# Stack loads in half as many transfers, and loads put in another order, in a two-layer decoder on one Trainium2 core

## What is computed

```python
x = ln(x + causal_attention(x))          # L0_attn
x = ln(x + cross_attention(x, ctx))      # L0_xattn: 1024 context tokens of 192 features per sequence
x = ln(x + soft_moe(x))                  # L0_ffn: 8 experts x 128 slots, 256 -> 1024 -> 256
x = ln(x + causal_attention(x))          # L1_attn
x = ln(x + cross_attention(x, ctx))      # L1_xattn
x = ln(x + block(x))                     # L1_ffn: own causal attention, then top-2 of 8 experts
```

## Time and profile before

| | us |
|---|---|
| median of 3 runs | 3067.17 (3059.79 to 3073.33) |
| profiled execution, its own time | 3064.33 |
| span of that execution, first to last instruction | 3062.5 |
| PE busy | 2568.9 |
| DVE busy | 1499.4 |
| ACT busy | 1346.1 |
| GpSimd busy | 457.8 |

### The profile page before, as it was taken

One profiled execution on the slowest core, in us unless ns is written; L12 is line 12 of the kernel. 1 busy time (PEld: TensorE's weight loads), 2 busy tenths in 40 slices (PEclk: granted clock), 3 DMA queues, 4 the chain that ended last, 5 costly groups with the idle time before them and its releaser, 6 DMA issues. The chain is left out here.

```text
span 3062.5 us, 48054 instructions
## 1 busy us (share of the span) xinstructions
PE 2568.9 (84%) x15793; PEld 1469.9 (48%) x15794; DVE 1499.4 (49%) x4196; ACT 1346.1 (44%) x2886; POOL 457.8 (15%) x719
## 2 busy tenths in 40 slices
PE   4999999999828979998588999898987986489992
PEld 2555544444314446676355544343434554356671
DVE  0555677888425420013444487777744564222223
ACT  2555456666634432211244456665754553022220
POOL 3222212101110000000112212212122000500004
PEclk7899999999969999999699999999998997599996
DMA  8344664454000012203644465354422332711102
GB/s 205 97 126 126 131 118 82 68 73 73 1 17 1 1 59 88 87 17 137 158 109 123 111 128 80 56 101 62 92 59 60 103 83 95 249 31 34 34 30 89
DMA packets 184550, 259.98 MB, mean 85 GB/s; under 512 B 32952, under 2 KB 106944, under 8 KB 184256
## 3 DMA queue, kind: packets, MB, share of 16 engines
q1 hardware_dynamic: 181264, 248.85, 34.5%
q0 software_dynamic: 3072, 8.39, 0.9%
HBM read 180.71 MB, written 81.53 MB: 86 GB/s over the span
## 5 line engine op out<-in xcount | busy, mean ns | idle before, releaser
L1345 ACT ACTIVATE second_p<-psum 128x512 f32<-128x512 f32 (+3 forms) x1024 | 461.7, 520 | 287.9 <-PE psum L1211 284.3
L1345 ACT ACTIVATE first_p<-psum 128x512 f32<-128x512 f32 (+3 forms) x768 | 365.7, 547 | 179.1 <-PE psum L1211 176.5
L1419 DVE TENSOR_REDUCE first_max_parts<-psum 128x1 f32<-128x512 f32 x512 | 323.0, 684 | 74.7 <-PE psum L1188 72.1
L1419 DVE TENSOR_REDUCE second_max_parts<-psum 128x1 f32<-128x512 f32 x512 | 321.9, 683 | 72.9 <-PE psum L1188 70.2
L1415 DVE CUSTOM_DVE_ANT_0 second_masked<-psum,mask_qk 128x384 f32<-128x384 f32 (+3 forms) x512 | 230.0, 489 | 230.7 <-PE psum L1188 189.1
L1201 PE MATMUL psum<-second_q,second_k 64*128 64x512 f32 (+3 forms) x1024 | 227.7, 440 | 42.1 <-DVE second_max_parts L1419 26.2
L1188 PE MATMUL psum<-second_k,second_q 64*128 64x512 f32 (+3 forms) x1024 | 203.7, 395 | 67.5 <-DMA second_k<-a_k_parts 51.5
L1223 PE MATMUL psum<-second_p,second_v_aug 128*32 128x512 f32 (+3 forms) x2048 | 240.1, 542 | 8.3 <-ACT second_p L1345 8.1
L1188 PE MATMUL psum<-first_k,first_q 64*128 64x512 f32 (+3 forms) x768 | 158.0, 411 | 61.7 <-ACT first_held L1382 26.0
L1201 PEld LDWEIGHTS psum<-second_q,second_k 64*128 64x128 f32 x1024 | 98.8, 188 | 230.1 <-issue 83.6
L1415 DVE CUSTOM_DVE_ANT_0 first_masked<-psum,mask_qk 128x128 f32<-128x128 f32 (+3 forms) x256 | 114.8, 488 | 179.7 <-PE psum L1188 152.5
(11 more groups left out here) (317 smaller groups left out, 3819.2 us busy)
## 6 DMA issues: line engine op xcount, KB each, us to landing
first_k<-c_k_parts SPq DMA_DIRECT2D x128, 128.0 KB, 5.7
second_q<-a_q_parts SPq DMA_DIRECT2D x256, 64.0 KB, 2.8
second_k<-a_k_parts SPq DMA_DIRECT2D x256, 64.0 KB, 2.9
second_k<-c_k_parts SPq DMA_DIRECT2D x128, 128.0 KB, 5.6
first_q<-a_q_parts SPq DMA_DIRECT2D x128, 64.0 KB, 2.9
first_k<-a_k_parts SPq DMA_DIRECT2D x128, 64.0 KB, 2.9
c_k_parts<-first_held SPq DMA_DIRECT2D x16, 512.0 KB, 3.2
first_q<-c_q_parts SPq DMA_DIRECT2D x128, 64.0 KB, 5.3
```

Of the source, the lines that this page charges most:

```text
L1345: evacuated(act.activation(probs[tile % 2][:, 2 * h + p, q0:SEQ], bank[:, q0:SEQ], ACT.Exp, scale=scale), event)
L1419: evacuated(v.reduce_max(max_parts[n % 2][:, h, p, qt, k0 // BANK:k0 // BANK + 1], bank[:, 0:width], axis=AX_X), event)
```

## The change

Three things. First, a stack is loaded in 8 transfers: one fills two blocks, that is 32 partitions. To make the two heads of a partition contiguous in DRAM, the columns of the q and k weights and biases are reordered on the host (`by_heads`), so that row 2d + i holds feature d of head i; a partition's run is then 2 x 512 or 2 x 1024 tokens in one piece. For q both blocks hold the same part, so the DRAM side repeats its 16 rows twice; for k the two blocks hold parts 0 and 1. `keys_of` views a causal stack's keys without a gap in the larger tile. Second, a `weights` event in the plan issues the weights at a chosen place: `first` issues its own weights ahead of the plan as before, and c0's weights after load 2; `second` issues all weights after its first four stacks; the first contexts come later. In `first`, load 1 to load 3 now stand behind slot 1's front pieces. Third, the experts' semaphore is split into `up_in` and `down_in`: PE and ACT wait for up and its bias first, PE waits for down at its second half, DVE for down.

```diff
@@ stage_attentions, SP
-                for dst, src, columns in own_loads:
-                    sp.dma_start(dst, src, allow_slow_non_contiguous=columns).then_inc(own_in, 16)
-                for dst, src, columns in later_loads:
-                    sp.dma_start(dst, src, allow_slow_non_contiguous=columns).then_inc(later_in, 16)
+                if not layers[0].projected:
+                    fetch_weights(own_loads, own_in)
...
                     for h in range(2):
                         row = b * D + h * P + g * 2 * HD
-                        for blk, (qp, kp) in enumerate(((0, 0), (0, 1), (1, 0), (1, 1))):
-                            at = slice(64 * h + HD * blk, 64 * h + HD * (blk + 1))
-                            sp.dma_start(qs[n % NB][at, :, :].bitcast(F32),
-                                         q_dram[qp, row:row + 2 * HD, :].rearrange("(i d) t -> d i t", d=HD)
+                        for half in range(2):
+                            at = slice(64 * h + 2 * HD * half, 64 * h + 2 * HD * (half + 1))
+                            sp.dma_start(qs[n % NB][at, :, :].bitcast(F32).rearrange("p i t -> p (i t)"),
+                                         q_dram[half, row:row + 2 * HD, :].rearrange("(d i) t -> d (i t)", i=2)
+                                         .unsqueeze(0).to_broadcast([2, HD, 2 * SEQ])
                                          ).then_inc(stack_in[n % NB], 16)
-                            sp.dma_start(ks[n % NB][at, :, 0:layer.keys].bitcast(F32),
-                                         k_dram[kp, row:row + 2 * HD, :].rearrange("(i d) t -> d i t", d=HD)
+                            sp.dma_start(ks[n % NB][at, :, :].rearrange("p i t -> p (i t)")[:, 0:2 * layer.keys].bitcast(F32),
+                                         k_dram[:, row:row + 2 * HD, :].rearrange("a (d i) t -> a d (i t)", i=2)
                                          ).then_inc(stack_in[n % NB], 16)
...
+                    elif event[0] == "weights":
+                        if layers[0].projected:
+                            fetch_weights(own_loads, own_in)
+                        fetch_weights(later_loads, later_in)
@@ stage_attentions, PE
-                        pe.wait_ge(stack_in[r], 256 * (n // NB + 1))
+                        pe.wait_ge(stack_in[r], 128 * (n // NB + 1))
@@ stage_experts
+                    pe.wait_ge(up_in[r], (pair + 1) * per_load)
                     for m in range(HM):
...
+                    pe.wait_ge(down_in[r], (pair + 1) * per_load)
                     for t in range(tiles):
@@ build
-        pieces = {-3: front_pieces(a0, 0, "x") + FIRST_LOADS, -2: front_pieces(a0, 1, "x")}
+        pieces = {-3: front_pieces(a0, 0, "x") + FIRST_LOADS[:2],
+                  -2: front_pieces(a0, 1, "x") + FIRST_LOADS[2:5] + [("weights", 0, 0), ("load", 3, 0)]}
...
-        contexts = {-3: [("context", BATCH, 0), ("context", BATCH + 1, 0)]}
+        contexts = {-1: [("context", BATCH, 0), ("context", BATCH + 1, 0)]}
...
-        pieces = {-3: FIRST_LOADS}
-        contexts = {-3: [("context", BATCH, 0), ("context", BATCH + 1, 0)]}
+        pieces = {-3: FIRST_LOADS + [("weights", 0, 0)]}
+        contexts = {-2: [("context", BATCH, 0), ("context", BATCH + 1, 0)]}
```

More of the change, by code:

```diff
@@ L977, in wait_weights, with keys_of @@
                 eng.wait_ge(later_in, 16 * len(later_loads))
+        def keys_of(n):
+            keys = layer_of(n).keys
+            return ks[n % NB][:, :, :].rearrange("p i t -> p (i t)")[:, 0:2 * keys].rearrange("p (i t) -> p i t", i=2)
         def pre_norm(slot):
@@ L994, in _, with fetch_weights @@
             def _(sp):
-                for dst, src, columns in own_loads:
-                    sp.dma_start(dst, src, allow_slow_non_contiguous=columns).then_inc(own_in, 16)
-                for dst, src, columns in later_loads:
-                    sp.dma_start(dst, src, allow_slow_non_contiguous=columns).then_inc(later_in, 16)
+                def fetch_weights(loads, done):
+                    for dst, src, columns in loads:
+                        sp.dma_start(dst, src, allow_slow_non_contiguous=columns).then_inc(done, 16)
+                if not layers[0].projected:
+                    fetch_weights(own_loads, own_in)
                 def context(slot):
@@ L1188, in unit @@
                         ins = pe.matmul(bank_of(event, h)[:, 0:width], qs[r][own, p, qt * P:(qt + 1) * P],
-                                        ks[r][own, p, k0:k0 + width], start=True, stop=True)
+                                        keys_of(n)[own, p, k0:k0 + width], start=True, stop=True)
                         filled(ins, event)
@@ L1200, in scores @@
                         own = slice(64 * h, 64 * h + 64)
-                        pe.matmul(bank_of(event, h)[:, q0:SEQ], ks[r][own, p, t * P:(t + 1) * P],
+                        pe.matmul(bank_of(event, h)[:, q0:SEQ], keys_of(n)[own, p, t * P:(t + 1) * P],
                                   qs[r][own, p, q0:SEQ], start=True, stop=False)
@@ L1563, in stage_experts @@
         hidden = sb("hidden", [P, HM, BANK])
-        w_in = [c.sem(f"{name}_w_in{i}") for i in range(2)]
+        up_in, down_in = [c.sem(f"{name}_up_in{i}") for i in range(2)], [c.sem(f"{name}_down_in{i}") for i in range(2)]
         s_up, s_gelu = c.sem(f"{name}_up"), c.sem(f"{name}_gelu")
         s_down, s_read = c.sem(f"{name}_down"), c.sem(f"{name}_read")
-        per_load = 16 * 4
+        per_load = 16 * 2
         tiles = BANK // P
@@ L1584, in body @@
                     one = bass.ds(e, 1)
-                    sp.dma_start(up[r][:, :, :], w1[one, :, :].rearrange("o (k p) n -> p (o k) n", p=P)).then_inc(w_in[r], 16)
-                    sp.dma_start(up_bias[r][:, :], b1[one, :, :].rearrange("o p m -> p (o m)")).then_inc(w_in[r], 16)
-                    sp.dma_start(down[r][:, :, :], w2[one, :, :].rearrange("o (m p) n -> p (o m) n", p=P)).then_inc(w_in[r], 16)
+                    sp.dma_start(up[r][:, :, :], w1[one, :, :].rearrange("o (k p) n -> p (o k) n", p=P)).then_inc(up_in[r], 16)
+                    sp.dma_start(up_bias[r][:, :], b1[one, :, :].rearrange("o p m -> p (o m)")).then_inc(up_in[r], 16)
+                    sp.dma_start(down[r][:, :, :], w2[one, :, :].rearrange("o (m p) n -> p (o m) n", p=P)).then_inc(down_in[r], 16)
                     wait_for(sp, s_read, tiles * (e - 1))
                     sp.dma_start(down_bias[r][:, :], b2[one, :].rearrange("o n -> (o n)").partition_broadcast(P)
-                                 ).then_inc(w_in[r], 16)
+                                 ).then_inc(down_in[r], 16)
                 for_experts(sp, body)
@@ L1596, in body @@
                 def body(e, pair, r):
-                    pe.wait_ge(w_in[r], (pair + 1) * per_load)
+                    pe.wait_ge(up_in[r], (pair + 1) * per_load)
                     for m in range(HM):
@@ L1617, in body @@
                 def body(e, pair, r):
-                    act.wait_ge(w_in[r], (pair + 1) * per_load)
+                    act.wait_ge(up_in[r], (pair + 1) * per_load)
                     wait_for(act, s_down, e * tiles)
@@ L1629, in body @@
                 def body(e, pair, r):
-                    v.wait_ge(w_in[r], (pair + 1) * per_load)
+                    v.wait_ge(down_in[r], (pair + 1) * per_load)
                     for t in range(tiles):
@@ L2289, in by_groups, with by_heads @@
     return np.concatenate([others, own], axis=-1)
+HEADED = {"L0_attn_w_attn": 2, "L0_attn_b_attn": 2, "L1_attn_w_qkv": 2}
+HEADED.update({f"{layer}_{x}": 1 for layer, names in (("L0_xattn", ("Wq", "Wk", "bq", "bk")), ("L1_xattn", ("wq", "wk", "bq", "bk")),
+                                                      ("L1_ffn", ("Wq", "Wk", "bq", "bk"))) for x in names})
+def by_heads(a, blocks):
+    own, rest = a[..., :blocks * D], a[..., blocks * D:]
+    own = own.reshape(own.shape[:-1] + (-1, 2, HD)).swapaxes(-2, -1).reshape(own.shape)
+    return np.concatenate([own, rest], axis=-1)
 def kernel(**inputs):
@@ L2303 @@
             a = by_groups(a, name in TURNED_ROWS)
+        if name in HEADED:
+            a = by_heads(a, HEADED[name])
         if name == "ctx_768":
```

## The result

The changed kernel takes 3908.4 us (median of 4 runs, 3904.2 to 3911.8), the kernel before beside it 3069.8 (4 runs, 3059.8 to 3073.3): 1.274 times as long, with a 95% interval from 1.270 to 1.277. The forecast was 3870, the range 3640 to 4150. The profiled execution took 3907.3 us, its span is 3905.6; that of before was 3062.5, so there are 843 us of span to explain.

A forecast was written before the change was run, and what follows sets the result against it. TensorE (PE), busy 84% of the span, was taken as the bound, then PE's own waits. Terms 281 + 300 + 85 + 70 + 26 + 28 + 22 - 4 = 808 on 3064 gave 3872, forecast 3870 us, range 3640 to 4150.

The forecast's parts named there:

- Two engines: Stack loads: with two entries outermost in DRAM, each transfer runs on two DMA engines at 25.1 GB/s each; forecast chance 0.60.
- L: Stack loads: time from a stack's first issue to its landing, priced at 22.8 us (causal) and 33.2 us (context).
- d: Attention steps: time from a unit's start to the next stack's first issue; 6.9, 3.5 or 2.1 us, summing to 146 and 150.
- The half clock, +85: Attention stretches: after standing, PE runs at clock 0.50, doubling its part of each step before the next issue, 1.2 x 70 us.
- The shared queue, +70: Attention stretches: stores and value loads ahead of stack loads in the same queue cost 40 and 30 us.
- The first start: First program's start: load 4 goes out at 139 instead of 113.44 us, +26.
- the experts' wait: First expert: PE no longer waits for the megabyte of down, -4 us of a 12.4 us wait.
- The ends: Ends of both attention programs: the last stacks land 10 and 12 us later, +22.
- The second start: Second program's start: load 4 at 1545 instead of 1516.23 us, +28; the fourth stack covers the widening's wait for weights.
- 16 engines: Rival for the stack loads: transfers dealt out finer, causal load 7.1 us instead of 11, total 2990 us; chance 0.08.
- Partly covered: Rival for the attention stretches: other engines catch up during the stall and the clock holds, total 3640 us; chance 0.15.
- slower still: Rival for the stack loads: stores behind whole stacks, late held tiles, 20 GB/s per engine, total 4120 us; chance 0.14.

The follow-up runs named there:

- the first experiment: The changed kernel with the 16 rows outermost in the DRAM pattern and the two copies or parts inside, same eight transfers and bytes: 2956.4 us, 0.963 of before.
- the run with k cut: The changed kernel with each k load cut into its two parts, 16 rows outermost, q loads left as two copies: 3300.8 us, 1.077 of before.
- the loads alone: The kernel before with the new eight stack loads and their q and k column order, without the new order of work and the experts' split: 3940.4 us, 1.283 of before.
- order alone: The kernel before with the new order of work and the experts' split, keeping the old 16 loads: 3037.2 us, 0.989 of before.
- the dose runs: The changed kernel, once with only q loads cut into two copies of 16 rows (3411.9 us), once with only k loads cut into two parts (3300.8 us).

## Why the prediction held, and where its terms did not

**Two engines** was right at its root: the share of 0.13, the landing 18 us after the last issue (3289.76 to 3307.9), and the first experiment, which differs in that alone. By the rule cited ahead (the Trainium skill, DMA: Bandwidth & Descriptors, Why a DMA increments its semaphore by 16 and not by 1) it is two; the trace agrees, with 0.13 = 2 / 16. The same page of the Trainium skill names the leading broadcast in its Rules for kernel authors; the run with k cut shows it, with the causal L at 15.3. Its advice to merge transfers under 64 KB, which the prediction drew on too, bears on these loads only at its edge, since they had 64 and 128 KB; what the merge is worth by itself is the 81 us on 16 engines.

**L** was priced at 22.8 and 33.2 and is 23.0 and 32.7. Summed over the stretches it is 773 us in the first (forecast 772) and 1149 in the second (1147).

**d was undersized.** Forecast: 146 and 150 us. Summed over the steps from the trace, the kernel before has 196 and 198, the kernel after 188 and 217. The step that failed is the choice of 6.9, 3.5 and 2.1 from three pairs of rows: single steps with pieces between reach 12.5 us (a projection) and 21.9 (turned rows) in the kernel before. It was 109 us too little.

**The half clock, +85, was mostly not on the path.** The clock did fall, from 0.97 and 0.94 in the two stretches to 0.81 and 0.80, and PE's busy time rose by 56 and 79 us. But where it falls shows in the windows of the turn above and of the next one's start:

```profile
3282.70:3285.30 2.60, 2.56 (x22) 1.86 (x22) 0.51 (x4) 0.60 (x1) 0.73 (x1) 0.50 0.00 0
3285.30:3296.50 11.20, 11.05 (x104) 6.60 (x100) 7.61 (x35) 5.49 (x15) 0.00 (x0) 0.83 0.15 54
3296.50:3307.90 11.40, 0.23 (x2) 0.00 (x0) 0.57 (x2) 1.09 (x2) 0.00 (x0) 0.62 0.13 52
3307.90:3311.00 3.10, 3.05 (x26) 2.35 (x26) 0.78 (x7) 0.98 (x2) 0.73 (x1) 0.50 0.00 1
```

PE had stood 4.75 us ahead of the first of these rows and 11.22 ahead of the last (the idle times in brackets above), and in both the granted clock is 0.50, which is 1.2 GHz. Of the slow work only the 2.6 us up to the next issue are in d (2.6 us instead of 2.1). The rest lies under the load, and PE still stands 11 us behind it. Over both stretches PE's busy time inside d rose by 27 us, and d itself by 11.

**The shared queue, +70, was not on the path either.** L's sums are the loads' own. It is the stores that stand behind the stacks: the page has 15.3 us from issue to landing for this store, 3.1 in the 16-engine version.

```profile
c_k_parts<-first_held SPq DMA_DIRECT2D x16, 512.0 KB, 15.3
```

In their place the second stretch has 50 us in which the stack was there and PE was not. So the sum of the stretches, 736, against 746 measured, is partly luck: 155 us of clock and queue that the path all but lacks, for 109 of d and 50 of PE's own work that it has.

**Starts and ends.** The first start is +26.6 (first load to load 4 and the earlier begin; forecast +26), the experts' wait -3.9 (-4). The ends were priced at 22, 10 for one program and 12 for the other, and are 33: from the last load's first issue to PE's last instruction of its program the first takes 123.0 us instead of 108.8, and from the second's last load to the end of the kernel it is 19 more (table). Up to the first unit on that last stack it is 12.4 and 12.9 us more (33.3 instead of 20.9, 22.8 instead of 9.9); where the other 8 arise was not followed up. The second start, from the first load of that program to load 4, is what failed: from 1452.06 it was 64.2, now 105.1, +41 instead of +28. The four stacks take 84.9 us, as priced; then 20.2 us pass until load 4 goes out, not 7. The step that failed says the fourth stack covers the widening's wait for the weights. It does not; GpSimd's first row there is

```profile
1899.32 1.41 POOL L1107 TENSOR_TENSOR second_v_aug<-second_v_raw,second_a_bv 128x256 f32<-128x256 f32 x2 [80.75 <-DMA second_a_wo<-in_L_attn_w_o]
```

right behind the fourth stack's landing at 1898.5, and PE, done with the earlier units, waits 19.3 us for it. Where the weights go first (the loads alone), load 4 goes out 9.8 us after the fourth stack has landed. With these the account closes: 27 + 746 + 41 + 33 - 4 = 843. Of the 35 us that the forecast of 808 lacks, 13 are the second start, 11 the ends and 10 the stretches.

**The rivals.** "16 engines" was priced at 2990 and, once made, took 2956. The starts together gave 40 us, as priced (38); the stretches gave 66, not 30. Half of the 66 shows as PE's shorter busy time, 17 and 15 us less at a clock of 1.00 and 0.96 instead of 0.97 and 0.94, which the forecast had not counted. That it decides at five engines, L below 11, fits what ran: a causal L of 10.5 gives 3037, 15 gives 3301 and 3412; five itself was not tried. "Partly covered" needed d at 2.1 everywhere and did not come; "slower still" needed 20 GB/s per engine, where the load's window has 26.5.

## What to carry to other kernels

Before merging transfers, count the entries of the outermost dimension: the same eight loads differ by 952 us with the two copies or the 16 rows outside. Here it was the DRAM side that was turned; the SBUF side kept its 32 partitions, and no run turned that. A load's price on the path is L + d wherever the next is issued only when the last has been used; sum d over all steps from the trace, not from three. A slower clock or a slower store counts only where the path runs through it; ask what PE would do with the time it gets back.

## What was not expected of the hardware

With the same 16 engines and the same bytes, the eight larger loads are quicker than the 16: L is 7.8 and 10.1 us (16 outermost) against 10.5 and 14.9 (order alone), and the DMA share of the first stretch is 0.40 against 0.51 at about the same rate, 108 and 103 GB/s. The order-alone kernel's windows:

```profile
90.00:719.70 629.70, 591.13 (x4277) 304.78 (x4279) 435.91 (x1126) 378.57 (x776) 125.97 (x190) 0.98 0.51 103
1481.60:2485.60 1004.00, 895.21 (x6560) 472.44 (x6558) 631.06 (x1862) 557.43 (x1165) 194.19 (x330) 0.93 0.42 91
```

For a causal load the issuing accounts for it, as the first rival had reckoned: from first to last issue it is 4.4 us instead of 7.4, and from there to the landing 2.8 against 2.9 (medians of the second program). For a context load this last part is shorter too, 5.6 us instead of 7.6. Beside the number of issues two things differ, 32 partitions per transfer instead of 16 and contiguous rows of 4 and 8 KB instead of 2 and 4; no run parts these. The lower end of the prediction's price, 8.6 GB/s per engine into 16 partitions, would also account for the missed L of the dose runs: 64 KB of k per engine at 8.6 are 7.6 us instead of 2.6, and 10.4 + 7.6 + 1.9 = 19.9, against 20.4 measured. The same price would make the causal L of both dose runs 10.4 + 3.8 + 1.9 = 16.1, above the measured 15.2 and 15.3, so it fits only in part. That was worked out, not tested.

The eight issues of a stack follow each other at 0.64 us (3285.30 to 3289.76 above, seven steps), those of before at 0.53, and it is no different with 16 engines: there a single issue takes 0.54 to 0.60 us, where one of the old takes as little as 0.30. With two engines the last issue of a stack mostly holds SP for 2 us or more (3289.76 above; over 1.5 us in 70 of 80 stacks, against 2 of 80 with 16 engines); what SP waits for there was not looked into.
